# All sixteen mask matmuls of a seven-product group in one place, two of the banks opened by their masks

## What is computed

```python
inter = xf @ c1_w.T @ c2_w.T                      # rank 16, 3584 scores for each token
blk = inter.reshape(B * T, 56, 64)
idx = argmax(blk, axis=-1) + arange(0, 3584, 64)  # one hidden unit out of each 64
h = relu(einsum('bkm,bm->bk', w1[idx], xf))
out = einsum('bk,bkm->bm', h, w2t[idx])
```

## Time and profile before

| | us |
|---|---|
| median of 3 runs (793.71 to 794.48) | 793.86 |
| the profiled execution | 794.16 |
| its span | 792.3 |
| TensorE matmuls busy | 785.7 (99%) |
| VectorE busy | 590.7 (75%) |
| GpSimd busy | 433.2 (55%) |
| ScalarE busy | 249.7 (32%) |

### The profile page before, as it was taken

The page is one execution under the profiler, slowest core; times in us unless marked ns, Lnnn a source line. Parts: engine busy times, 40 slices in busy tenths (PEclk is TensorE's granted clock), DMA queues, the critical chain, the costliest instruction groups (busy, mean ns, idle before and its releaser), DMA issues.

```text
span 792.3 us, 11474 instructions
## 1 busy us (share of the span) xinstructions
PE 785.7 (99%) x3883; PEld 641.2 (81%) x3888; DVE 590.7 (75%) x962; ACT 249.7 (32%) x375; POOL 433.2 (55%) x265
## 2 busy tenths in 40 slices
PE   8999999999999999999999999999999999999998
PEld 8888987478888888888888888888888888888886
DVE  6655669887884878887877778787878787777864
ACT  6457666973321130312121221303031212212030
POOL 3935898576999954545445252535454543525240
PEclk9999999999999999999999999999999999999999
DMA  9126402000111110111111111111111121111104
GB/s 340 66 106 212 164 19 89 8 1 8 60 54 60 37 49 29 54 60 53 60 53 60 53 60 53 58 34 37 43 53 60 53 60 53 60 53 53 53 18 195
DMA packets 22615, 53.22 MB, mean 67 GB/s; under 512 B 4544, under 2 KB 6592, under 8 KB 22464
## 3 DMA queue, kind: packets, MB, share of 16 engines
q1 hardware_dynamic: 22448, 51.86, 18.9%
q10 hardware_dynamic: 144, 1.05, 0.4%
HBM read 48.70 MB, written 4.19 MB: 67 GB/s over the span
## 4 chain that ended last, share of the span: by engine, by line
PE 96%; DVE 2%; DMA 1%; issue 0%; ACT 0%; SPq 0%; DVEq 0%
PE bank L1770 13%; PE bank L1771 13%; PE bank L1772 13%; PE bank L1675 12%; PE bank L1677 11%; PE bank L1676 11%; PE bank L1488 4%; PE bank L1490 4%; PE bank L1489 4%; PE bank L1629 3%; PE bank L1684 2%; PE bank L1666 2%; DMA x<-x_in 1%; PE bank L1645 1%; PE bank L1504 1%; DVE xT_lo L1070 1%
## 5 line engine op out<-in xcount | busy, mean ns | idle before, releaser
L1770 PE MATMUL bank<-w_hi,h_hi 128*128 128x512 f32 x448 | 176.2, 393 | 0.0
L1771 PE MATMUL bank<-w_lo,h_hi 128*128 128x512 f32 x448 | 175.0, 391 | 0.0
L1772 PE MATMUL bank<-w_hi,h_lo 128*128 128x512 f32 x448 | 174.4, 389 | 0.0
L1277 DVE TENSOR_TENSOR x<-bank,x 128x512 f32<-128x512 f32 x208 | 133.5, 685 | 50.0 <-PE bank L1772 50.0
L564 POOL TENSOR_TENSOR lo_r<-r,slot 128x512 fp32r<-128x512 f32 x52 | 67.5, 1299 | 155.9 <-ACT slot L787 155.9
L1772 PEld LDWEIGHTS bank<-w_hi,h_lo 128*128 128x128 f32 x448 | 84.1, 188 | 18.0
L1770 PEld LDWEIGHTS bank<-w_hi,h_hi 128*128 128x128 f32 x448 | 84.1, 188 | 15.7
L1771 PEld LDWEIGHTS bank<-w_lo,h_hi 128*128 128x128 f32 x448 | 84.4, 188 | 15.2
L1675 PE MATMUL bank<-xT_hi,slot 128*128 128x512 f32 x240 | 95.0, 396 | 0.0
L1676 PE MATMUL bank<-xT_lo,slot 128*128 128x512 f32 x240 | 93.5, 390 | 0.0
L1677 PE MATMUL bank<-xT_hi,lo_r 128*128 128x512 f32 x192 | 74.8, 390 | 0.0
(11 more groups left out here) (205 smaller groups left out, 1599.5 us busy)
## 6 DMA issues: line engine op xcount, KB each, us to landing
r<-w SPq DMA_DIRECT2D x56, 256.0 KB, 3.5
w_raw<-w SPq DMA_DIRECT2D x28, 512.0 KB, 4.0
x<-x_in SPq DMA_DIRECT2D x8, 512.0 KB, 10.0
ctx_raw<-ctx_in SPq DMA_DIRECT2D x8, 512.0 KB, 3.5
xn<-ctx_in SPq DMA_DIRECT2D x8, 512.0 KB, 4.8
out<-x SPq DMA_DIRECT2D x7, 512.0 KB, 2.7
W_raw<-wqkv SPq DMA_DIRECT2D x6, 512.0 KB, 10.5
c_raw<-c SPq DMA_DIRECT2D x112, 16.0 KB, 2.0
```

The lines of the kernel that those rows point to most:

```text
L1277: nc.vector.tensor_tensor(x[:, t, c], bank[unit_banks(g)[p]][:, :], x[:, t, c], ALU.add).then_inc(unit_added, 1)
L1770: nc.tensor.matmul(dst, h_hi[:, j, m], w2_hi[:, j, c], start=j == 0, stop=False)
L1771: nc.tensor.matmul(dst, h_hi[:, j, m], w2_lo[:, j, c], start=False, stop=False)
L1772: last = nc.tensor.matmul(dst, h_lo[:, j, m], w2_hi[:, j, c], start=False, stop=j == GJ - 1)
```

## The change

The four masks of block (0,0) stay where they are, and all the others move up right behind them. Blocks (0,1) and (1,0) no longer get their masks on top of the product: the masks open the banks (the first has the start flag, the last has no stop flag), and the products 6 and 7 accumulate onto them and close them. The waits for u4 and for p1's copy move with the masks. `hid_done` now counts (0,0), (1,1), (0,1), (1,0), where it counted (0,0), (0,1), (1,1), (1,0), so VectorE's waits for the second and third are swapped; VectorE's order of work is kept. The number of matmuls is the same.

```diff
             def make_c12(g):
-                dve.wait_ge(hid_done, g * 4 + 2)
+                dve.wait_ge(hid_done, g * 4 + 3)
                 add_sum(bank[2][:, :], 2, u4)
             def make_c22(g):
-                dve.wait_ge(hid_done, g * 4 + 3)
+                dve.wait_ge(hid_done, g * 4 + 2)
                 dve.wait_ge(sum_done, summed(g, "c12"))
                 add_sum(bank[1][:, :], 1, v22)
...
+            def opening_mask(g, r, b):
+                for i in range(TB):
+                    nc.tensor.matmul(bank[c_bank(g, r, b)][:, i * P:(i + 1) * P],
+                                     pick[:, TB * b + i, r * P:(r + 1) * P], floor_b[:, :], start=i == 0, stop=False)
...
                 product(bank[4][:, :], slot0, lo_r12, B21, True)
                 hidden_mask(g, 0, 0)
+                pe.wait_ge(sum_done, summed(g, "u4"))
+                hidden_mask(g, 1, 1, alone=True)
+                opening_mask(g, 0, 1)
+                pe.wait_ge(p1_copied, fast(g, 1, 0))
+                opening_mask(g, 1, 0)
                 hidden_bank(g, 3)
                 cut_ready(4)
                 pe.wait_ge(T_lo_done, 8)
                 product(bank[3][:, :], slot1, lo_r21, (T_hi[3], T_lo[3]), True, True).then_inc(prod_done, 1)
                 cut_ready(5)
-                pe.wait_ge(sum_done, summed(g, "u4"))
-                product(bank[2][:, :], slot2, lo_r11, B22, True)
-                hidden_mask(g, 0, 1)
-                hidden_mask(g, 1, 1, alone=True)
+                product(bank[2][:, :], slot2, lo_r11, B22, False, True).then_inc(hid_done, 1)
                 cut_ready(6)
-                pe.wait_ge(p1_copied, fast(g, 1, 0))
-                product(bank[0][:, :], slot0, lo_r22, (T_hi[4], T_lo[4]), True)
-                hidden_mask(g, 1, 0)
+                product(bank[0][:, :], slot0, lo_r22, (T_hi[4], T_lo[4]), False, True).then_inc(hid_done, 1)
```

## The result

The changed kernel takes 799.25 us (median of 4 runs) against 793.98 us: a ratio of 1.0069 with the interval 1.0054 to 1.0084. It is slower by 5.3 us, where 4.7 was forecast (798.5 us); the measured time lies inside the range, 795.8 to 800.8.

What follows compares the result with a forecast made beforehand. TensorE's queue was taken as the bound. Per group, 0.57 us of standing less 0.18 saved by merged bursts gives +0.39; over twelve groups +4.7 us, 793.86 to 798.5 us, range 795.8 to 800.8.

Steps and rivals of the forecast that it cites:

- Bound: Whole kernel: TensorE's queue sets a group's time, 43.05 us; the change acts by matmul distances or a wait there.
- Bursts merged: Mask bursts on TensorE: sixteen masks in one burst cost 1.03 us, not 1.21; saves 0.18 per group, 2.2 over twelve.
- Rival 3: Burst of sixteen masks: long burst is slow, 0.29 us more per group, 802 us; chance 0.05.
- The moved waits: Waits for u4 and p1's copy, moved behind the (0,0) masks: no price, 1.1 us in hand at the least.
- Rival 4: Masks behind (0,0): u4 is late and twelve masks stand until VectorE makes it; above 800 us; chance 0.02.
- The tail: Products 6 and 7 and first output unit: unit waits for VectorE, TensorE stands 0.57 us once a group.
- L: Start of the last matmul of product 6, from which the tail's times are counted.
- hand-over: From VectorE's end of (1,1)'s lo part to the first unit's weight load: 0.20 us taken, bounds 0.07 and 0.23.
- margin: Original, before the first output unit: 0.23 us between the lo part's end (336.29) and first weight load (336.52).
- The range's lower end: 795.8 us: a hand-over without any delay and a cheap burst.
- Rivals 1 and 2: First unit: no stall, merge alone counts, 791.7 us, chance 0.08; or stall about 0.2 us cancels merge, 794.0, chance 0.05.
- Rival 1: First unit: merge alone counts, no stall, if lo parts are done by L + 2.5 to 2.7; 791.7 us; chance 0.08.

Runs made afterwards that it cites:

- one more instruction: Changed kernel plus an unused VectorE row maximum over 128x512 between c22 and the lo part of (0,1), in each of twelve groups: 804.69 us.
- c12 shortened: Changed kernel with c12's sum done for 32 of its 512 columns only, so the output differs: 793.59 us.
- the four-burst kernel: Kernel with (1,1) first on VectorE, its sixteen masks in four bursts of four instead of one burst: 795.09 us.
- the original's bursts, (1,1) first: Original with its bursts of 4, 8, 4 kept, block (1,1) first in the eight and first on VectorE and ScalarE: 794.26 us.
- kernel with (1,1) first: Changed kernel with block (1,1) taken ahead of (0,1) on VectorE and ScalarE, c22 right behind v22: 791.62 us.

## Why the prediction was right, step by step

*Bound.* TensorE's queue set the time, and a wait in it went to the end undiminished: 0.45 us more of chain gave 5.4 us (one more instruction), 0.5 less took 5.7 (c12 shortened).

*Bursts merged.* Forecast 1.03 us for sixteen and 0.18 saved per group; measured 1.01 and 0.20 (the period of 42.85 against 43.05), 2.4 us over twelve groups where 2.2 were forecast. The fixed price of a burst, read as 0.09 from four against eight masks, is 0.10 by the four-burst kernel. Rival 3, a long burst that grows dear, is dead: the second eight of the sixteen take 0.42 to the next product's start (328.26 to 328.68), 0.05 each. The 81 ns that the Trainium skill gives for a sustained stream of such pairs ("TensorE: Matmul & The Clock Gate", section "Back-to-back issue gap") aren't seen in sixteen in a row either: they cost less, by the rows above 0.05 to 0.06 each.

*The moved waits.* No idle stands ahead of the masks in the changed kernel's list, as forecast. Rival 4 is dead.

*The tail.* Forecast to the lo parts' end L + 3.21, measured L + 3.22; load to second matmul 0.34 and 0.34. The one term that was mis-sized is the hand-over: 0.20 taken, 0.23 measured, which is the forecast's upper bound. With it TensorE loses 0.62 and not 0.57 us. So a group costs 0.62 - 0.20 = 0.42, as the period of the group above says (43.47 - 43.05), and twelve of them 5.0 of the 5.3 us. The twelve periods from the first unit of group 1 to that of group 13 come to 521.77 us, where the original has 516.64: 5.1 us. They aren't all alike. Two groups, of 43.53, have a hand-over of 0.28 and not 0.23, the last one of 0.05; why the two differ is not shown.

One reading of the prediction was too kind: it called the 0.23 us between the earlier trace rows a margin. The changed kernel needs the same 0.23 when TensorE does stand. So in the loop's groups the original had next to no margin. It didn't stand either: with 0.28 us from the lo parts to the load (the original's bursts, (1,1) first) and with 0.73 (four bursts) the first unit starts the same 0.21 behind the start of its burst of four masks as with 0.23. In the last group, whose waits are against constants, the hand-over of the changed kernel took 0.05 or 0.06 (lo parts through at 772.24, load at 772.30):
```profile
770.79 1.45 DVE L1218 SCALAR_TENSOR_TENSOR h_lo<-bank,h_hi 128x512 fp32r<-128x512 f32 x2
```
```profile
772.30 0.19 PEld L1776 LDWEIGHTS bank<-w_hi,h_hi 128*128 128x128 f32 x1 [0.66 <-DVE h_lo L1218]
```

The range's lower end has a slip: its own terms give +1.7 us, 795.5 from the median, and 795.8 is reached only from the profiled execution's 794.16. The measured time is far from it.

*Rivals 1 and 2.* The stall did come, so 791.7 us was not seen here; but it is the time of the kernel in which VectorE takes the early block first (791.62). Rival 1's condition, lo parts by L + 2.5 to 2.7, is borne out: at L + 2.48 there is no idle, and with c12 shortened, at L + 2.71, 0.12. The saving that rival 1 counted is real, and the change hid it behind its own wait.

The kernel with (1,1) first is the version that beats both: 791.62 us, 0.3% below the original (ratio 0.9959 to 0.9981) and 7.6 us below the change.

## What to carry to other kernels

Before work is taken out from between a producer and a wait on a saturated engine, count what that work was covering: lay the consumer's chain (start to end, hand-over, exposed load) against what is left of the queue from the same instant. When a result is made ready earlier on one engine, move it forward in the order of the next engine too, or it waits behind the one that is now last. And of several waits on register values in a row, try the one that comes last at the end, when the engine is found standing there; in the group whose waits are against constants this gained nothing.

One more way lies in the source and no run tried it. The first three matmuls of the first unit (j = 0) read block (0,1) alone, and yet the wait ahead of them is for the lo part of (1,1) too. With a wait for (0,1) there and one for (1,1) ahead of the fourth matmul, the chain would have three steps more, 0.68 us. As an estimate from the rows: the fourth matmul's turn is at L + 16 x 0.227 = L + 3.63, its weight load's 0.22 earlier at L + 3.41 (a load that isn't held starts that much ahead of its matmul, 336.52 against 336.74 in the kernel with (1,1) first), and the lo part of (1,1) with its hand-over is there at L + 3.22 + 0.23 = L + 3.45. So at most some hundredths of idle would be left in the changed order too.

## What the runs showed of the hardware that was not expected

- A wait that is followed by other waits on register values held TensorE's next weight load 0.23 us behind the releasing instruction's end, though all the others had been met; as the last of them it took 0.05. In the one group with waits against constants it was the other way round, 0.05 with the late wait first and 0.12 with it last. The page "Advanced Engine Details and Errata" of the Trainium skill, section "Network/Comms", gives 50 to 100 ns for one read of a semaphore, and 0.23 against 0.05 fits some steps of that kind in series; which of them costs what, no run here separates.
- A burst of 128-column bf16 matmuls within 512-column float32r ones has a fixed price of 0.10 us, whether its masks are added on top or stand alone (masks that open a bank came only inside a longer burst, where they cost what the others do); 4, 8, 12 and 16 masks cost 0.33, 0.56, 0.77 and 1.01 us. The profile shows the fixed part as the 0.32 step behind a burst; that it is the float32 weight load of 0.19 us, which a short matmul doesn't cover, is argued and not shown.
- A VectorE instruction whose follower doesn't depend on it cost 0.60 us where its record says 0.69 (336.19 to 336.79), and 0.61 where it says 0.70 (c12 at 334.22 in the kernel with (1,1) first): records of independent neighbours overlap by some 0.09.
